# Packing an adjacency matrix on TensorE: 16 columns of whole words, with the rows of a group dealt in another order

## Chip, cores, metric

One core of one Trainium2 chip runs the whole program. The metric is the device time of one execution in microseconds (us). The profiled execution is a separate one, taken with the hardware profiler; its span runs from the first to the last instruction.

## What is computed

Four graph attention layers over N = 8192 nodes with 128 features and one adjacency matrix `adj` of 8192 x 8192 int32 (256 MiB). Each layer normalises x, takes `relu`, and adds an attention output. The first:

```python
h = jnp.maximum(_layernorm(x, axis=-1), 0.0)
Wh = h @ W
e = (Wh @ a1)[:, None] + (Wh @ a2)[None, :]
e = jnp.where(e >= 0, e, ALPHA * e)
scores = jnp.where(adj > 0, e, NEG_BIG)
attention = jax.nn.softmax(scores, axis=1)
x = x + attention @ Wh
```

Layers 1 and 3 end in `elu`. Layer 2 also drops attention weights under 1e-4 and scales by the number of valid neighbours of a row, `L = valid.sum(axis=1)`: this is where the kernel needs degrees of rows.

## The kernel before

**Tiling.** Rows are taken in 16 groups of 512 (`GROUPS`), columns in 64 tiles of 128 (`KT`), which form 4 chunks of 16 tiles (`CHUNKS`, `JC`). For each group and tile VectorE makes q, 128 columns by 512 rows of unnormalised weights (L780), from a mask, and TensorE multiplies four blocks of it with `vals` (128x129, f32) into `acc` (L1240). TensorE runs these products in program order, chunk after chunk, in all four layers.

**The bits.** `adj` is read once, in layer 0, as 512 pieces of 512 KB. From then on the adjacency lies in SBUF as `bits`, one uint16 word for 16 rows of a group: word w (0 to 31, `WORDS`) of column c holds bit b (`PLANES`, 0 to 7) in each of two bytes o, which stands for row 64b + 2w + o of the group. VectorE unpacks a chunk of bits into the byte mask with eight shifts (`planes`, L753).

**How a piece becomes bits.** A piece is 128 rows and 1024 columns (`PT` = 8 tiles). Four pieces (h, o) give the 512 rows of a group over 1024 columns: `adj_pieces` has row 256h + 2p + o on partition p.
1. `load_piece` on SyncE (L432) brings it to one of four slots of `adj_int` (`ADJ_RING`), once ScalarE has read the piece that was there four pieces ago. SyncE issues these loads in the order of pieces, with loads of r and of x, and stores of x, in between (`transfers_and_pieces`).
2. `binary` on ScalarE (L1341) writes 0 or 1 as a byte. Pieces o = 0 and o = 1 interleave, so two of them make one 128x1024 array of 16-bit values, read as f16, in one of four slots of `adj_pairs` (`BIN_RING` / 2). The same instruction sums the row of the piece (`accum_out`), which gives the degree by partition. It may start when the pairs up to eight pieces back are packed.
3. `pack` on TensorE (L1154) multiplies each 128x128 tile of a pair (weights) with the packer. The packer for h is 128x32: row 32m + w has 2^(4h+m) in column w, m = 0 to 3. So a piece of h = 0 gives bits 0 to 3, one of h = 1 bits 4 to 7, and they add up in the same 32 columns of `ps_pack`. A pack is a chunk, 8 pieces: 4 pairs of 8 tiles, 32 matmuls. It waits for each pair as it comes.
4. `words` on ScalarE (L1348) copies `ps_pack` out as uint16.

**What sets the order.** `pack(*ahead(v, c))` stands after chunk c of group v and packs two chunks ahead (`LEAD`); in group 0 packs stand at hand-picked tiles (`FIRST_PACKS`). The last one, of group 15 chunk 3, stands after chunk 1 of group 15; chunks 2 and 3 follow it. TensorE waits in its own order, so a pack whose pair is late holds the chunks behind it.

**Degrees.** `turn_degrees` on SyncE, in layer 1 ahead of the transfers of group 4, writes the 128x64 degrees to DRAM in order of rows (L492), waits, and reads them back by tile (L495). They are read in layer 2. The packer is filled by eight `affine_select` on GpSimd at the start and cleared after the last pack; layer 2 then uses its 128x128 zeros as `nothing`.

Of the kernel before, what the change touches and what calls it, by code (L numbers as in the profile page):

```python
# [7 lines left out]
P = 128  # L8
F = 128
N = 8192  # L10
BLOCKS = 4
# [6 lines left out]
WORDS = W // 16  # L18
# [4 lines left out]
PT = 8  # L23
# [8 lines left out]
PLANES = 8  # L32
# [127 lines left out]
def build(nc, x, adj, ws, avs, out):  # L160
# [11 lines left out]
    wh2 = nc.dram_tensor("wh_of_layer_2", (N, F), F32).ap()  # L172
    rows = nc.dram_tensor("rows", (LAYERS, KT, P), F32).ap()
    rows_by_group = rows.rearrange("k (g b) p -> k g (b p)", b=BLOCKS)
    adj_pieces = adj.rearrange("(g h p o) (k c) -> g k h o p c", h=2, p=P, o=2, c=PT * P)
    degree_rows = nc.dram_tensor("degree_rows", (N,), F32).ap()

    with ExitStack() as ctx:
# [26 lines left out]
        h_total = sb("h_total", [P, 1], F32)  # L205
        h_mean = sb("h_mean", [P, P], F32)
        threshold = sb("threshold", [P, 1], F32)
        packer = sb("packer", [P, BLOCKS, WORDS], F16)
        mean = sb("mean", [P, F], F32)
        s = sb("s", [P, 2, KT + 1], F32)  # L210
        smax = sb("smax", [P, 1], F32)
# [79 lines left out]
        mask_of_unit = flat(adj_int).bitcast(BF16)[:, 0:TRIP * P].rearrange("p (t i) -> p t i", i=P)  # L291
        q_of_unit = flat(q)[:, 0:TRIP * P].rearrange("p (n i) -> p n i", i=P)
        kept_of_unit = flat(q).bitcast(U8)[:, 8 * TRIP * P:9 * TRIP * P].rearrange("p (t i) -> p t i", i=P)
        nothing = packer[:, :, :].rearrange("p b w -> p (b w)")
        counts_of_unit = acc[0][:, 0, F + 1:F + 2]
        r_of_unit, tau_of_unit = rrow[:, 0, 0:P], rrow[:, 0, P:2 * P]

# [124 lines left out]
        def _(sp):  # L422
# [66 lines left out]
            def turn_degrees():  # L489

                sp.wait_ge(degree_ready, 1)
                sp.dma_start(degree_rows.rearrange("(h p o) -> p h o", p=P, o=2),  # L492
                             degree[:, :].rearrange("p (h o) -> p h o", o=2)).then_inc(degree_out, 16)
                sp.wait_ge(degree_out, 16)
                sp.dma_start(degree[:, :], degree_rows.rearrange("(t p) -> p t", p=P), allow_slow_non_contiguous=True)\  # L495
                    .then_inc(degree_in, 16)

# [49 lines left out]
        @block.gpsimd  # L547
        def _(pool):
            nc.gpsimd.memset(ident[:, :], 0.0).then_inc(ident_ready, 1)
            pool.wait_ge(ident_ready, 1)  # L550
            nc.gpsimd.affine_select(out=ident[:, :], in_=ident[:, :], compare_op=ALU.not_equal, fill=1.0,
                                    base=0, pattern=[[-1, P]], channel_multiplier=1).then_inc(ident_ready, 1)
            nc.gpsimd.memset(packer[:, :, :], 0.0).then_inc(consts_ready, 1)
            nc.gpsimd.memset(ones[:, :], 1.0).then_inc(consts_ready, 1)
            nc.gpsimd.memset(threshold[:, :], -0.5).then_inc(consts_ready, 1)
            nc.gpsimd.memset(wh1[:, :, F], 1.0).then_inc(consts_ready, 1)
            pool.wait_ge(consts_ready, 4)
            step = 4
            for h in range(2):
                for m in range(4):  # L560
                    nc.gpsimd.affine_select(out=packer[:, h, :], in_=packer[:, h, :], compare_op=ALU.not_equal,
                                            fill=float(2 ** (4 * h + m)), base=-WORDS * m,
                                            pattern=[[-1, WORDS]], channel_multiplier=1).then_inc(consts_ready, 1)
                    step += 1
                    pool.wait_ge(consts_ready, step)

            for c in range(CHUNKS):
                pool.wait_ge(norm_scales, c + 1)
                for n in range((c + 1) * JC - BLOCKS, (c + 1) * JC):
                    last = nc.gpsimd.tensor_scalar(x_rows_0[:, n, :], x_rows_0[:, n, :], rs_0[:, n:n + 1],  # L570
                                                   nm_0[:, n:n + 1], ALU.mult, ALU.add)
                last.then_inc(norm_by_pool, 1)

            starts = [WHOLE[0], SOON[1], LATE[1], SOON[2], LATE[2]]
            for n, to in enumerate([scales(st)[0][:, :] for st in starts] + [found[:, 0:1], found[:, 1:2], S[:, :]]):
                pool.wait_ge(smax_ready, n + 1)
                nc.gpsimd.partition_all_reduce(to, smax[:, :], P, RMAX).then_inc(S_ready, 1)
                if n == LATE[1].n:
                    for t in range(KT):
                        nc.gpsimd.memset(number[:, t:t + 1], float(t + 1)).then_inc(numbered, 1)  # L580
                    pool.wait_ge(adj_packed, GROUPS * PIECES)
                    nc.gpsimd.memset(packer[:, :, :], 0.0).then_inc(nothing_ready, 1)

        @block.vector
        def _(dve):
# [548 lines left out]
        def _(pe):  # L1134
# [11 lines left out]
            def pack(v, c):  # L1146
# [3 lines left out]
                for i in range(0, QP, 2):  # L1150
                    pe.wait_ge(adj_binary, v * PIECES + (c * QP + i + 2))
                    for t in range(PT):
                        at = (i // BLOCKS * PT + t) * WORDS
                        last = nc.tensor.matmul(ps_pack[:, at:at + WORDS],  # L1154
                                                adj_pairs[:, i % BIN_RING // 2, t * P:(t + 1) * P],
                                                packer[:, i % BLOCKS // 2, :], start=(i == 0 and t == 0),
                                                stop=(i == QP - 2), skip_group_check=True)
                    last.then_inc(adj_packed, 2)

# [519 lines left out]
```

## Time and profile before

| | us |
|---|---|
| median of 3 runs | 3884.77 |
| lowest, highest | 3883.24, 3884.99 |
| the profiled execution | 3884.23 |
| its span | 3882.4 |
| TensorE busy in it | 3819.8 |
| VectorE busy in it | 3570.3 |

The profiled execution has 1.8 us outside its span. Layer 0 takes the first 1055 us or so, the other three layers the rest. Busy time of TensorE counts overlapping matmuls once; durations of single matmuls (176 ns for a pack's) are longer than the distance between their starts, so costs of TensorE are read from the chain or from the distance of starts.

### The profile page before, as it was taken

The numbers are of one execution on the slowest core, as the hardware profiler recorded it, in microseconds if no ns is written. First come the engines' busy times: TensorE is split into PE (matmuls) and PEld (weight loads), VectorE is DVE, ScalarE is ACT, GpSimd is POOL, SyncE is SP. The second block draws the span as 40 slices with busy tenths as digits, with TensorE's granted clock in tenths as the row PEclk, the third lists the DMA queues.
The fourth block names the chain that finished last, engine by engine and source line by source line (L and its number), as shares of the span: only waits on it lengthen the run. The fifth ranks groups of instructions, "written<-read, shape, count | busy, mean of one in ns | idle before, by whom it ended". The sixth has DMA issues, their size and how long they took to land.

```text
span 3882.4 us, 83778 instructions
## 1 busy us (share of the span) xinstructions
PE 3819.8 (98%) x35555; PEld 3810.9 (98%) x35555; DVE 3570.3 (92%) x7790; ACT 1187.1 (31%) x2492; POOL 17.0 (0%) x107
## 2 busy tenths in 40 slices
PE   7999999999999999999999999999997999999999
PEld 6999999999999999999999999999997999999999
DVE  7888989888899999999999999999997999999998
ACT  6766767676631111111133121121122000000000
POOL 1000000000000000000000000000000000000000
PEclk9999999999999999999999999999998999999999
DMA  7888888888401200000002000000000000000000
GB/s 236 294 289 284 286 282 287 286 279 284 146 18 23 18 20 20 18 20 20 15 15 67 18 20 20 18 20 20 18 17 12 17 12 15 17 12 18 15 18 9
DMA packets 207144, 340.05 MB, mean 88 GB/s; under 512 B 56624, under 2 KB 131504, under 8 KB 206768
## 3 DMA queue, kind: packets, MB, share of 16 engines
q1 hardware_dynamic: 205040, 334.41, 27.3%
q8 instruction: 279, 4.57, 0.5%
q14 instruction: 97, 0.79, 0.1%
q10 hardware_dynamic: 1728, 0.27, 0.0%
HBM read 305.57 MB, written 21.20 MB: 84 GB/s over the span
## 4 chain that ended last, share of the span: by engine, by line
PE 95%; ACT 2%; DVE 2%; DMA 1%; issue 0%; ACTq 0%; SPq 0%; DVEq 0%
PE acc L1240 92%; PE ps_pack L1154 1%; PE ps_wh L1258 1%; ACT vals L1436 1%; DVE q L780 1%; ACT adj_pairs L1341 0%; DMA vals<-in_x_dram 0%; PE ps_wh L1252 0%; DVE mask L753 0%; PE acc L1222 0%; DMA adj_int<-in_adj_dram 0%; PE ps_bc L1198 0%; DMA adj_int<-adj_int 0%; PE acc L1177 0%; ACT xnew L1448 0%
## 5 line engine op out<-in xcount | busy, mean ns | idle before, releaser
L1240 PE MATMUL acc<-vals,q 128*128 128x129 f32 (+1 forms) x32576 | 3671.9, 275 | 5.2 <-DVE q L780 5.1
L1240 PEld LDWEIGHTS acc<-vals,q 128*128 128x128 f32 x32576 | 3653.9, 192 | 6.9 <-issue 5.2
L780 DVE SCALAR_TENSOR_TENSOR q<-rrow,R,mask 128x512 f32<-128x512 f32 x3968 | 2825.7, 745 | 172.0 <-PE acc L1240 28.7
L1341 ACT ACTIVATE adj_pairs<-adj_int,threshold 128x1024 uint8<-128x1024 int32 x512 | 585.3, 1146 | 243.9 <-PE ps_pack L1154 143.1
L753 DVE TENSOR_SCALAR mask<-bits 128x512 uint16<-128x512 uint16 x2048 | 435.9, 285 | 7.4 <-DMA rrow<-rows 4.2
L1448 ACT ACTIVATE xnew<-acc,rec 128x128 f32<-128x128 f32 x244 | 69.3, 366 | 854.6 <-DVE rec L818 760.5
L1455 ACT ACTIVATE e<-xnew 128x512 f32<-128x512 f32 x47 | 29.7, 631 | 405.5 <-DVE xnew L849 317.2
L1468 ACT ACTIVATE e<-xnew,nm,rs 128x128 f32<-128x128 f32 x193 | 79.4, 481 | 214.2 <-DVE nm L625 214.2
L1515 ACT ACTIVATE wh<-ps_wh 128x512 f32<-128x512 f32 x48 | 28.7, 598 | 339.9 <-PE ps_wh L1258 339.8
L1463 ACT ACTIVATE sd<-ve 128x4 f32<-128x4 f32 (+1 forms) x49 | 9.9, 202 | 365.6 <-DVE ve L606 365.5
L849 DVE SCALAR_TENSOR_TENSOR xnew<-mean,none,xnew 128x128 f32<-128x128 f32 x188 | 64.9, 345 | 51.2 <-ACT xnew L1448 51.2
L1341 ACT ACTIVATION_READ_ACCUMULATOR adj_pairs<-adj_int,threshold 128x1 f32 x512 | 97.4, 190 | 0.0
L780 DVE SCALAR_TENSOR_TENSOR q<-rrow,tau,mask 128x512 f32<-128x512 f32 x112 | 79.8, 744 | 3.3 <-PE acc L1240 1.6
L1481 ACT ACTIVATE hT<-adj_int 128x512 uint16<-128x512 uint16 x60 | 42.2, 770 | 105.7 <-DMA adj_int<-adj_int 105.7
L1154 PEld LDWEIGHTS ps_pack<-packer,adj_pairs 128*128 128x128 f16 x2048 | 60.8, 96 | 0.9
L1154 PE MATMUL ps_pack<-packer,adj_pairs 128*128 128x32 f16 x2048 | 61.3, 176 | 0.0
L1258 PE MATMUL ps_wh<-w_sb,hT 128*128 128x130 f32 x386 | 52.7, 280 | 2.4 <-ACT hT L1502 1.8
L592 DVE BATCH_NORM_STATS2 stats<-xnew 128x6 f32<-128x128 f32 x193 | 54.4, 283 | 0.1
L1258 PEld LDWEIGHTS ps_wh<-w_sb,hT 128*128 128x128 f32 x386 | 48.0, 195 | 3.3 <-ACT hT L1502 2.5
L1463 ACT ACT_TABLE_LOAD x35 | 44.9, 1283 | 0.6
L1436 ACT ACTIVATE vals<-wh,D 128x129 f32<-128x129 f32 (+1 forms) x128 | 38.0, 393 | 3.7 <-DVE D L713 1.9
L1348 ACT ACTIVATE bits<-ps_pack 128x512 uint16<-128x512 f32 x64 | 36.8, 575 | 0.0
(228 smaller groups left out, 743.9 us busy)
## 6 DMA issues: line engine op xcount, KB each, us to landing
adj_int<-in_adj_dram SPq DMA_DIRECT2D x512, 512.0 KB, 4.9
rrow<-rows SPq DMA_DIRECT2D x60, 256.0 KB, 3.3
x_between_layers<-xnew SPq DMA_DIRECT2D x32, 256.0 KB, 3.4
xin<-x_between_layers SPq DMA_DIRECT2D x32, 256.0 KB, 2.8
xin<-in_x_dram SPq DMA_DIRECT2D x16, 256.0 KB, 5.2
wh_of_layer<-wh SPq DMA_DIRECT2D x1, 4096.0 KB, 16.7
x_of_layer<-xnew SPq DMA_DIRECT2D x16, 256.0 KB, 2.3
xin<-x_of_layer SPq DMA_DIRECT2D x16, 256.0 KB, 2.8
```

The source lines that it names most:

```text
L592: st.did(nc.vector.bn_stats(stats[:, b, :], xnew[:, b, :]))
L753: last = nc.vector.tensor_scalar(mask_words[:, buf, :, b, :], words, amount, ONES, op, ALU.bitwise_and)
L780: nc.vector.scalar_tensor_tensor(q[:, j % RING, :], row, column(R_, t), mask[:, c % 2, j, :], ALU.max, ALU.mult).then_inc(q_ready, 1)
L849: last = nc.vector.scalar_tensor_tensor(o[:, b, :], mean[:, :], none4[:, b:b + 1], o[:, b, :], ALU.mult, ALU.add)
L1154: last = nc.tensor.matmul(ps_pack[:, at:at + WORDS], adj_pairs[:, i % BIN_RING // 2, t * P:(t + 1) * P], packer[:, i % BLOCKS // 2, :], st ...
L1240: last = nc.tensor.matmul(to, q[:, j % RING, b * P:(b + 1) * P], vals[:, t, 0:width(g.layer)], start=first, stop=(t == KT - 1 or g.two and ...
L1258: last = nc.tensor.matmul(projected[:, b // 2, b % 2, :], hT[:, b, :], w_sb[:, g.layer + 1, :], start=True, stop=True)
L1341: nc.scalar.activation(adj_bytes[:, n % BIN_RING // 2, :, n % 2], adj_int[:, n % ADJ_RING, :], ACT.Sign, bias=threshold[:, 0:1], accum_out ...
L1436: last = nc.scalar.activation(vals[:, t, 0:n], wh1[:, t, 0:n], ACT.Copy, scale=scales(st)[4][:, t:t + 1])
L1448: last = nc.scalar.activation(o[:, b, :], acc[g.parity][:, b // 2, at:at + F], ACT.Copy, scale=by[:, b:b + 1])
L1463: nc.scalar.activation(sd[:, m], ve[:, m], ACT.Sqrt).then_inc(sd_ready[g.to], 1)
L1468: last = nc.scalar.activation(h[:, b, :], xnew[:, b, :], ACT.Relu, bias=nm[:, b:b + 1], scale=rs[:, b:b + 1])
```

## The change

A pack matmul streams one packer of 16 columns, `packer[:, 0:16]`, for either h: row 16m + w has 2^m in column w, m = 0 to 7. For that a piece must hold all eight bits of a word: `adj_pieces` now puts row 64m + 32h + 2w + o on partition 16m + w. A piece of h = 0 fills words 0 to 15, one of h = 1 words 16 to 31, each with its eight bits; the two no longer add up in the same columns. The bits in SBUF are the same as before. The load's source is now three dimensions, 8 by 16 by 1024, where it was 128 by 1024. Degrees lie on other partitions, so they are written to DRAM by 16 transfers, each of 16 partitions. The packer's array keeps 128 columns for `nothing`.

```diff
@@ -172,7 +172,8 @@
     wh2 = nc.dram_tensor("wh_of_layer_2", (N, F), F32).ap()
     rows = nc.dram_tensor("rows", (LAYERS, KT, P), F32).ap()
     rows_by_group = rows.rearrange("k (g b) p -> k g (b p)", b=BLOCKS)
-    adj_pieces = adj.rearrange("(g h p o) (k c) -> g k h o p c", h=2, p=P, o=2, c=PT * P)
+
+    adj_pieces = adj.rearrange("(g m h w o) (k c) -> g k h o m w c", m=PLANES, h=2, w=WORDS // 2, o=2, c=PT * P)
     degree_rows = nc.dram_tensor("degree_rows", (N,), F32).ap()
 
     with ExitStack() as ctx:
...
@@ -489,9 +490,13 @@
             def turn_degrees():
 
                 sp.wait_ge(degree_ready, 1)
-                sp.dma_start(degree_rows.rearrange("(h p o) -> p h o", p=P, o=2),
-                             degree[:, :].rearrange("p (h o) -> p h o", o=2)).then_inc(degree_out, 16)
-                sp.wait_ge(degree_out, 16)
+                rows_of_plane = degree_rows.rearrange("(g m h w o) -> m w g h o", m=PLANES, h=2, w=WORDS // 2, o=2)
+                for m in range(PLANES):
+                    for h in range(2):
+                        sp.dma_start(rows_of_plane[m, :, :, h, :],
+                                     degree[m * (WORDS // 2):(m + 1) * (WORDS // 2), :]
+                                     .rearrange("p (g h o) -> p g h o", h=2, o=2)[:, :, h, :]).then_inc(degree_out, 16)
+                sp.wait_ge(degree_out, 16 * PLANES * 2)
                 sp.dma_start(degree[:, :], degree_rows.rearrange("(t p) -> p t", p=P), allow_slow_non_contiguous=True)\
                     .then_inc(degree_in, 16)
 
...
@@ -550,19 +555,19 @@
             pool.wait_ge(ident_ready, 1)
             nc.gpsimd.affine_select(out=ident[:, :], in_=ident[:, :], compare_op=ALU.not_equal, fill=1.0,
                                     base=0, pattern=[[-1, P]], channel_multiplier=1).then_inc(ident_ready, 1)
-            nc.gpsimd.memset(packer[:, :, :], 0.0).then_inc(consts_ready, 1)
+            nc.gpsimd.memset(packer[:, :], 0.0).then_inc(consts_ready, 1)
             nc.gpsimd.memset(ones[:, :], 1.0).then_inc(consts_ready, 1)
             nc.gpsimd.memset(threshold[:, :], -0.5).then_inc(consts_ready, 1)
             nc.gpsimd.memset(wh1[:, :, F], 1.0).then_inc(consts_ready, 1)
             pool.wait_ge(consts_ready, 4)
             step = 4
-            for h in range(2):
-                for m in range(4):
-                    nc.gpsimd.affine_select(out=packer[:, h, :], in_=packer[:, h, :], compare_op=ALU.not_equal,
-                                            fill=float(2 ** (4 * h + m)), base=-WORDS * m,
-                                            pattern=[[-1, WORDS]], channel_multiplier=1).then_inc(consts_ready, 1)
-                    step += 1
-                    pool.wait_ge(consts_ready, step)
+            half = packer[:, 0:WORDS // 2]
+            for m in range(PLANES):
+                nc.gpsimd.affine_select(out=half, in_=half, compare_op=ALU.not_equal, fill=float(2 ** m),
+                                        base=-WORDS // 2 * m, pattern=[[-1, WORDS // 2]],
+                                        channel_multiplier=1).then_inc(consts_ready, 1)
+                step += 1
+                pool.wait_ge(consts_ready, step)
 
             for c in range(CHUNKS):
                 pool.wait_ge(norm_scales, c + 1)
...
@@ -1150,10 +1155,10 @@
                 for i in range(0, QP, 2):
                     pe.wait_ge(adj_binary, v * PIECES + (c * QP + i + 2))
                     for t in range(PT):
-                        at = (i // BLOCKS * PT + t) * WORDS
-                        last = nc.tensor.matmul(ps_pack[:, at:at + WORDS],
+                        at = (i // BLOCKS * PT + t) * WORDS + i % BLOCKS // 2 * (WORDS // 2)
+                        last = nc.tensor.matmul(ps_pack[:, at:at + WORDS // 2],
                                                 adj_pairs[:, i % BIN_RING // 2, t * P:(t + 1) * P],
-                                                packer[:, i % BLOCKS // 2, :], start=(i == 0 and t == 0),
+                                                packer[:, 0:WORDS // 2], start=(i == 0 and t == 0),
                                                 stop=(i == QP - 2), skip_group_check=True)
                     last.then_inc(adj_packed, 2)
 
```

SyncE in layer 0, from the start of the program. A row is one instruction or several alike: line, operation, destination<-source, size of the destination. Before:

```order
L425 DMA vals<-in_x_dram 128x16x128 x2
L432 DMA adj_int<-in_adj_dram 128x1024 x4
L425 DMA vals<-in_x_dram 128x16x128 x2
L432 DMA adj_int<-in_adj_dram 128x1024 x12
L446 DMA xin<-in_x_dram 128x4x128
L432 DMA adj_int<-in_adj_dram 128x1024 x12
```

And now:

```order
L426 DMA vals<-in_x_dram 128x16x128 x2
L433 DMA adj_int<-in_adj_dram 128x1x1024 x4
L426 DMA vals<-in_x_dram 128x16x128 x2
L433 DMA adj_int<-in_adj_dram 128x1x1024 x12
L447 DMA xin<-in_x_dram 128x4x128
L433 DMA adj_int<-in_adj_dram 128x1x1024 x12
```

No load has moved; each has a dimension more, since its source has three.

SyncE in layer 1, ahead of group 4 (`adj_int` serves there as room for a transpose of x). Before:

```order
L446 DMA xin<-x_between_layers 128x4x128
L459 DMA_TRANSPOSE adj_int<-adj_int 128x8x128
L492 DMA degree_rows<-degree 128x32x2
L495 DMA degree<-degree_rows 128x64x1
L469 DMA rrow<-rows 128x512
L450 DMA x_between_layers<-xnew 128x4x128
```

And now:

```order
L447 DMA xin<-x_between_layers 128x4x128
L460 DMA_TRANSPOSE adj_int<-adj_int 128x8x128
L496 DMA degree_rows<-degree 16x16x2 x16
L500 DMA degree<-degree_rows 128x64x1
L470 DMA rrow<-rows 128x512
L451 DMA x_between_layers<-xnew 128x4x128
```

One transfer has become 16 in the same place.

TensorE in a group of layer 0, packs between chunks. Before:

```order
L1154 MATMUL ps_pack<-packer,adj_pairs 128x32 x32
L1240 MATMUL acc<-vals,q 128x129 x64
L1154 MATMUL ps_pack<-packer,adj_pairs 128x32 x32
L1240 MATMUL acc<-vals,q 128x129 x64
L1154 MATMUL ps_pack<-packer,adj_pairs 128x32 x32
```

And now:

```order
L1159 MATMUL ps_pack<-packer,adj_pairs 128x16 x32
L1245 MATMUL acc<-vals,q 128x129 x64
L1159 MATMUL ps_pack<-packer,adj_pairs 128x16 x32
L1245 MATMUL acc<-vals,q 128x129 x64
L1159 MATMUL ps_pack<-packer,adj_pairs 128x16 x32
```

The places and counts are the same, the width is 16 in place of 32. (An f32 matmul of the program runs as two on the engine, so the profile counts 128 for a chunk.)

## Rows read from the trace of the kernel before

**Rows 1.** The page: busy us, share and instructions by engine; 40 slices in tenths

```profile
span 3882.4 us, 83778 instructions
PE 3819.8 (98%) x35555; PEld 3810.9 (98%) x35555; DVE 3570.3 (92%) x7790; ACT 1187.1 (31%) x2492; POOL 17.0 (0%) x107
...
PE   7999999999999999999999999999997999999999
...
DMA  7888888888401200000002000000000000000000
GB/s 236 294 289 284 286 282 287 286 279 284 146 18 23 18 20 20 18 20 20 15 15 67 18 20 20 18 20 20 18 17 12 17 12 15 17 12 18 15 18 9
```

**Rows 2.** The page: the chain that ended last, shares by engine and by line

```profile
PE 95%; ACT 2%; DVE 2%; DMA 1%; issue 0%; ACTq 0%; SPq 0%; DVEq 0%
PE acc L1240 92%; PE ps_pack L1154 1%; PE ps_wh L1258 1%; ACT vals L1436 1%; DVE q L780 1%; ACT adj_pairs L1341 0%; DMA vals<-in_x_dram 0%; PE ps_wh L1252 0%; DVE mask L753 0%; PE acc L1222 0%; DMA adj_int<-in_adj_dram 0%; PE ps_bc L1198 0%; DMA adj_int<-adj_int 0%; PE acc L1177 0%; ACT xnew L1448 0%
```

**Rows 3.** Busy by stretch: layers 0 and 3 (us, engines, clock, DMA, GB/s)

```profile
core 0: us, PE busy (x) PEld busy (x) DVE busy (x) ACT busy (x) POOL busy (x), PEclk, DMA share, GB/s
300.00:420.00 120.00, 120.00 (x1270) 119.90 (x1269) 105.36 (x236) 84.16 (x158) 0.00 (x0) 1.00 0.85 286
...
3000.00:3116.00 116.00, 116.00 (x1041) 116.00 (x1040) 112.31 (x227) 4.80 (x12) 0.00 (x0) 1.00 0.05 15
```

**Rows 4.** The chain in layer 0 in order of time (start, duration, what)

```profile
310.64 0.79 PE ps_pack L1154 x32
311.43 14.39 PE acc L1240 x128
325.82 0.79 PE ps_pack L1154 x32
326.62 14.39 PE acc L1240 x128
```

**Rows 5.** Waits from 300 to 900 us (total, times, longest), SyncE's apart

```profile
ACT adj_pairs L1341 <- DMA adj_int<-in_adj_dram: 60.0, 44, 2.4
...
SPq L432 <- ACT adj_pairs L1341: 475.6, 309, 4.8
```

**Rows 6.** Matmuls of one moving column: line's durations in ns, and the timeline

```profile
L1298 PEld LDWEIGHTS acc<-adj_pairs,adj_int x4: 95/95/98, 2941.8 to 2941.9; 128*128 128x128 bf16 x4
L1298 PE MATMUL acc<-adj_pairs,adj_int x4: 163/164/177, 2941.8 to 2941.9; 128*128 128x1 bf16 x4
...
2941.79 0.17 PEld L1298 LDWEIGHTS acc<-adj_pairs,adj_int 128*128 128x128 bf16 x4 [2.72 <-ACT adj_int L1620]
2941.80 0.25 PE L1298 MATMUL acc<-adj_pairs,adj_int 128*128 128x1 bf16 x4 [2.43 <-ACT adj_int L1620]
```

**Rows 7.** Busy by stretch where the DMA engines are full

```profile
12.00:16.00 4.00, 1.63 (x7) 1.23 (x7) 3.64 (x20) 0.81 (x2) 0.90 (x5) 1.00 1.02 403
...
90.00:100.00 10.00, 10.00 (x116) 9.99 (x116) 10.00 (x17) 6.98 (x12) 0.00 (x0) 1.00 0.98 367
...
310.00:311.00 1.00, 1.00 (x27) 0.99 (x27) 0.86 (x4) 0.07 (x1) 0.00 (x0) 1.00 1.01 401
```

**Rows 8.** Busy by stretch where layer 0's products begin: granted clock before DMA

```profile
60.00:70.00 10.00, 8.73 (x83) 8.75 (x84) 9.63 (x15) 6.45 (x12) 0.00 (x0) 0.71 0.60 212
```

**Rows 9.** Timeline of SyncE's queue at the start (start, us until the last)

```profile
22.86 31.60 SPq L432 DMA_DIRECT2D adj_int<-in_adj_dram  x12
54.50 1.17 SPq L446 DMA_DIRECT2D xin<-in_x_dram  x1
61.49 19.20 SPq L432 DMA_DIRECT2D adj_int<-in_adj_dram  x12
```

**Rows 10.** Timeline of TensorE at the last pack

```profile
1025.60 0.95 PE L1154 MATMUL ps_pack<-packer,adj_pairs 128*128 128x32 f16 x32
1026.38 3.76 PEld L1240 LDWEIGHTS acc<-vals,q 128*128 128x128 f32 x33
```

**Rows 11.** Timeline of SyncE's queue around the degrees in layer 1

```profile
1272.67 0.36 SPq L492 DMA_DIRECT2D degree_rows<-degree  x1
1287.26 0.36 SPq L495 DMA_DIRECT2D degree<-degree_rows  x1
1287.67 4.99 SPq L469 DMA_DIRECT2D rrow<-rows  x1
1309.81 0.38 SPq L450 DMA_DIRECT2D x_between_layers<-xnew  x1
```

**Rows 12.** Loads and binary steps of the pieces: ns min/median/max, landing

```profile
L432 SPq DMA_DIRECT2D adj_int<-in_adj_dram x512: 327/328/4735, 4.3 to 1014.0; - x171
...
DMA to landing us min/median/max: 3.5/4.9/10.2
...
L1341 ACT ACTIVATE adj_pairs<-adj_int,threshold x512: 1134/1142/1292, 21.6 to 1021.4; 128x1024 uint8<-128x1024 int32 x171
```

More of the change, by code:

```diff
@@ L207, in build @@
         threshold = sb("threshold", [P, 1], F32)
-        packer = sb("packer", [P, BLOCKS, WORDS], F16)
+        packer = sb("packer", [P, P], F16)
         mean = sb("mean", [P, F], F32)
@@ L293, in build @@
         kept_of_unit = flat(q).bitcast(U8)[:, 8 * TRIP * P:9 * TRIP * P].rearrange("p (t i) -> p t i", i=P)
-        nothing = packer[:, :, :].rearrange("p b w -> p (b w)")
+        nothing = packer[:, :]
         counts_of_unit = acc[0][:, 0, F + 1:F + 2]
@@ L581, in _ @@
                     pool.wait_ge(adj_packed, GROUPS * PIECES)
-                    nc.gpsimd.memset(packer[:, :, :], 0.0).then_inc(nothing_ready, 1)
+                    nc.gpsimd.memset(packer[:, :], 0.0).then_inc(nothing_ready, 1)
         @block.vector
```

## The prediction

> **What bounds the kernel now.** I read the page first. TensorE is busy 98% of the span, VectorE 92%, and the 40 slices show two parts: in the first ten the DMA engines are busy eight tenths and move about 285 GB/s, after that almost nothing [rows 1]. The chain that ended last is 95% TensorE, and the 2048 pack matmuls are 1% of it [rows 2]. The table by stage says the same: in layer 0 (300 to 420 us) TensorE is busy all the time at full clock, with DMA at 0.85; in layer 3 TensorE is as busy, with DMA at 0.05 [rows 3]. The chain inside layer 0 is nothing but TensorE: a chunk of 128 matmuls takes 14.39 us, a pack of 32 takes 0.79 us [rows 4]. So layer 0 is bound by TensorE, with the stream of adjacency pieces not far behind. The waits show how far: ScalarE waits 60.0 us in 600 for a piece to land, TensorE for none, and SyncE waits 475.6 us for a free slot of the ring [rows 5]. The edit therefore has two prices that count: what a pack costs TensorE, and what a piece costs the DMA engines.
>
> **Part 1, half the columns in a pack.** The number of instructions stays (64 packs of 32 matmuls). A pack is all on the path: 0.79 us / 32 = 24.7 ns from start to start, 64 x 0.79 = 50.6 us in total. Nothing in the trace shows 16 columns of f16. The nearest rows: four matmuls of bf16 weights with one moving column take 0.25 us, the last of them 0.164 us of it, so (0.25 - 0.164) / 3 = 29 ns apart, and their weight loads (0.17 - 0.095) / 3 = 25 ns apart [rows 6]. One column is no cheaper than 32, so what fixes the pitch is not the columns. The other end is that half the columns take half the time: 25.3 us less. I take zero, because the one-column row is the nearer to 16 columns than any proportion is; 0 to -25.3 us is the bound. The Trainium skill ("TensorE: Matmul & The Clock Gate", "Wait — 56ns, not 53.3ns?") has a floor of about 25 ns between starts however few the columns; by that rule this part is worth nothing, while streaming 16 columns less at 2.4 GHz, which is what it counts above the floor, would be 6.7 ns x 2048 = 13.7 us (an estimate).
>
> **Part 2, the dealing of rows.** Each piece is the same 128 rows of 4 KB, and the 512 loads stay where they stand on SyncE. What changes is the form of the load: the source was one dimension of 128 rows by 1024 elements, and is now 8 by 16 by 1024; the built program shows it on the destination, which becomes 128x1x1024. The transfer must be dealt to the 16 DMA engines by some count. If it goes by the 128 partitions, as it can have done before, nothing changes. If it goes by the outermost count that both sides share, only 8 engines get rows, 16 rows each. The trace of before holds no load with an outermost count under 64, so it prices neither; the bounds are zero and the price of 8 engines. I take the 8, since the two sides no longer have the same shape, 8 is the outer count of one of them, and a dealer that wants equal shares on both sides can make 8 and no more. The Trainium skill ("DMA: Bandwidth & Descriptors", "Why a DMA increments its semaphore by 16 and not by 1") states just this: the largest number up to 16 that divides the slowest dimension of both sides, here 8; no row of before can show it, and by any other dealing this part would cost nothing.
>
> The price: 512 KB is 524,288 bytes. With the engines full they move 401 to 403 GB/s (the microsecond after a pack, and 12 to 16 us), a little less at 90 to 100 us: 0.98 and 367 [rows 7]. Half of 401 is 200.5 GB/s, so a piece takes **2.615 us**. A chunk needs eight pieces, 20.9 us, and the other traffic (rows of x, r and the stores: 0.05 of 58 us in a group without pieces, 2.9 us a group [rows 3]) adds 0.7 us: 21.6 us for a chunk. TensorE needs 14.39 + 0.79 = 15.2 us for one. So the DMA engines become the bound of layer 0, and TensorE waits some 6 us in every pack. Such pauses cost clock: after the pause before 60 us the granted clock is 0.71 over ten microseconds [rows 8], that is 5.8 us at the lower level (1.2 of 2.4 GHz), 2.9 us lost. 15.2 + 2.9 = 18.1 us is still under 21.6, so this is hidden in each chunk but the last. ScalarE needs 8 x 1.14 us for a chunk's pieces [rows 12] and is no bound. The ring keeps the engines fed: with TensorE waiting in the pack, all of the next pieces are allowed, and up to four loads stand in the queue.
>
> The sum for layer 0: SyncE has issued 16 pieces by 54.5 us and the 17th goes out at 61.49 us [rows 9]. The 16 take 16 x 2.615 = 42 us and x another 10.5 us, just done by then; for projections that wait on ScalarE behind a late piece I add 4 us (bounds 0 to 10). From 65.5 us: 496 x 2.615 = 1297 us, 16 x 2.9 = 46 us of other traffic, 2 us to land, 1.3 us to make the piece binary, and its pair is packed: 1412 us. Today the last pack starts at 1025.6 and is over at 1026.4 us [rows 10]. In the program's order two chunks follow the last pack in either kernel, and everything behind them is unchanged. So **+386 us, and 3 us** for the cold start of those two chunks.
>
> **Part 3, the rest.** The degrees go out with 16 small transfers in place of one; together they move the same 4096 runs of 8 bytes. SyncE issues at 0.36 us each, so some 6 us more (10 us if an issue is slower). Behind them stand, on SyncE, the load of degrees back, the load of r for group 5 and the store of group 3. Today the first goes out at 1272.67 us, the next store at 1309.81 us: 22 us are free after the load of r at 1287.67 us, and that row is wanted only when the next group begins, about 55 us later [rows 11]. Cost zero; with the cover gone it would be at most 10 us once. Degrees themselves are read in layer 2. A load that needs a longer issue than the 0.328 us of today [rows 12] is hidden too: there are 512 in 1010 us, one in 1.97 us. The packer is made by eight selects on GpSimd as before, each of 16 columns and not 32. Unpacking reads the same words in the same places.
>
> Total against the profiled execution: span 3882.4 + 386 + 3 = 4271 us, with 1.8 us outside the span **4273 us**. That execution (3884.23) stands 0.5 us under the median of the runs, so the prediction needs no shift.
>
> **The rivals.** (a) *Sixteen engines, no gain*: the load is dealt by partitions, pack pitch stays at 24.7 ns. Then nothing on the path changes: 3884 us. For it speaks that the partitions are still 128; against it the mismatch of shapes. (b) *Not slower but faster*: sixteen engines, and the pitch follows the columns. 64 packs at 0.40 us are 25.3 us less, 3859 us; it decides from 0.2% (7.8 us), when a matmul falls under 21 ns. Against it is the one-column row. (c) *Slower with sixteen engines*: the new order of rows hits the memory worse. A piece has 1.97 us, and DMA is busy 0.85 of it, so it costs nothing until transfers are 18% slower, and 10 us for each per cent beyond (512 x 1.97 / 100). Both orders are rows of 32 KB at even steps over most of a group, so I see no reason. (d) *Eight engines at another rate.* If they keep the mean of the busy stretch, 286 / 0.85 / 16 = 21.0 GB/s each, a piece is 3.12 us and the total 4523 us; at 367 GB/s over 0.98 it is 2.80 us and 4365 us; if eight engines disturb each other less than sixteen, 2.45 us gives 4191 us. This is the forecast's own width.
>
> **How the numbers follow.** Eight engines 0.84 (within 4190 to 4460 us: 0.80), (a) 0.12, (b) 0.03, (c) 0.01. The predicted time is that of eight engines. The range is 4190 to 4460 us, and what it leaves out is (a), (b), (c) and the slowest rate of (d). About 0.2% can be told from no change here. Faster 0.03, same 0.12, slower 0.85.
>
> **What would show it.** In the profile after: layer 0 in 14 slices of 40 and not 10; DMA busy there about 0.5 as a mean of sixteen, near 200 GB/s; SyncE's loads 7 us or more to landing, not 4.9; ScalarE waiting for pieces for hundreds of us, TensorE waiting in line L1159 for ScalarE. Pack matmuls 24 to 25 ns apart wherever a pack runs unbroken. Layers 1 to 3 as long as before. Wrong if DMA stays at 0.85 and 285 GB/s (then (a)), or if a pack takes 0.4 us (then (b)).

## The result, and the profile after

| | before | after |
|---|---|---|
| median us (4 runs each) | 3884.88 | 4317.8 |
| lowest, highest | 3883.24, 3885.22 | 4298.87, 4353.05 |
| the profiled execution | 3884.23 | 4298.87 |
| its span | 3882.4 | 4297.1 |

The change makes the kernel slower: ratio 1.1126, 95% interval 1.1104 to 1.1149. The forecast was 4273 us in a range of 4190 to 4460 us.

The page of the kernel after: span, busy time, slices of 107 us each, and the chain that ended last. It answers to [rows 1] and [rows 2].

```profile
span 4297.1 us, 83793 instructions
PE 3956.7 (92%) x35555; PEld 3940.0 (92%) x35555; DVE 3573.6 (83%) x7790; ACT 1217.8 (28%) x2492; POOL 16.8 (0%) x107
...
PE   5778888888777999999999999999999799999999
...
PEclk8898889988888999999999999999999899999999
DMA  5555555555555201000000110000000000000000
...
PE 64%; DMA 28%; issue 3%; ACT 3%; DVE 1%; SPq 0%; ACTq 0%; DVEq 0%
```

TensorE is no longer the whole chain: 28% of it is DMA, where it was 1%. Layer 0 fills thirteen and a half slices, and in them the DMA engines are busy five tenths, not eight. A mean of 0.5 that never rises is what eight full engines out of sixteen look like.

The trace also has a record of every packet of the DMA engines, and a row of a piece is one packet of 4 KB. From 300 to 900 us of the kernel after, eight such packets are under way at once in 72% of the time, and seven to nine in 94%. A packet takes 159 ns in the median, and so it does in the kernel before, which has fifteen to seventeen under way in 58% of the time. One engine thus moves 4096 bytes in 159 ns, 25.8 GB/s, in either kernel; what is new is that only about eight engines carry rows at any moment. No record says which engines they are.

The stretch from 300 to 900 us (columns as in [rows 3]), the waits in it (total, times, longest), and one wait of the whole run:

```profile
300.00:900.00 600.00, 493.06 (x4590) 489.15 (x4587) 384.34 (x842) 317.81 (x569) 0.00 (x0) 0.90 0.53 207
...
ACT adj_pairs L1346 <- DMA adj_int<-in_adj_dram: 283.4, 218, 2.5
...
PE ps_pack L1159 <- ACT adj_pairs L1346: 98.8, 28, 5.1
```

```profile
PE ps_pack L1159 <- ACT adj_pairs L1346: 251.9, 67, 6.1
```

The DMA engines move 207 GB/s in place of 285. ScalarE waits 283.4 us for pieces in these 600 us, where it waited 60.0 in the same stretch of [rows 5]. TensorE waits for ScalarE in the pack, 67 times in the whole run, 3.8 us in the mean; before it did not wait there.

What ScalarE does in one chunk shows the rhythm in which pieces land (its timeline; the bracket is the idle time before, and what ended it):

```profile
521.73 1.15 ACT L1346 ACTIVATE adj_pairs<-adj_int,threshold 128x1024 uint8<-128x1024 int32 x1 [0.79 <-DMA adj_int<-in_adj_dram]
...
524.24 1.15 ACT L1346 ACTIVATE adj_pairs<-adj_int,threshold 128x1024 uint8<-128x1024 int32 x1 [1.27 <-DMA adj_int<-in_adj_dram]
...
526.75 1.15 ACT L1346 ACTIVATE adj_pairs<-adj_int,threshold 128x1024 uint8<-128x1024 int32 x1 [1.27 <-DMA adj_int<-in_adj_dram]
...
530.24 1.15 ACT L1346 ACTIVATE adj_pairs<-adj_int,threshold 128x1024 uint8<-128x1024 int32 x1 [2.24 <-DMA adj_int<-in_adj_dram]
```

Two pieces are mostly 2.51 us apart, now and then longer, as the 3.49 us here. Some of the longer gaps fall where rows of x or r are loaded; this one does not (between the pieces the packet records hold none of either), and its cause is not shown. 524,288 bytes in 2.51 us are 209 GB/s, 26 GB/s for each of eight engines.

The loads by line, to set beside [rows 12], and TensorE's timeline at the last pack, beside [rows 10]:

```profile
L433 SPq DMA_DIRECT2D adj_int<-in_adj_dram x512: 596/596/4617, 4.2 to 1426.7; - x171
```

```profile
1435.16 0.75 PE L1159 MATMUL ps_pack<-packer,adj_pairs 128*128 128x16 f16 x24
...
1437.50 0.36 PE L1159 MATMUL ps_pack<-packer,adj_pairs 128*128 128x16 f16 x8 [1.59 <-ACT adj_pairs L1346]
1437.71 4.60 PE L1245 MATMUL acc<-vals,q 128*128 128x129 f32 x25
```

The last pack is over at 1437.7 us, 411.3 us later than in [rows 10]. From there to the end it is 2859.4 us, before 2856.0. So all of the loss but 3.4 us is in layer 0, ahead of the last pack. The pack also shows how a late pair looks: 24 matmuls run at once, the eight of the last pair 1.59 us later.

### The profile page after: what moved, and what is told of

Same layout as the page of the kernel before. It is cut to its first block, busy times and chain, and to the rows that moved or that the text cites. A ratio compares the mean times of both kernels' runs of the same rounds, so it can differ in the third digit from the quotient of the medians.

```text
span 4297.1 us, 83793 instructions
## 1 busy us (share of the span) xinstructions
PE 3956.7 (92%) x35555; PEld 3940.0 (92%) x35555; DVE 3573.6 (83%) x7790; ACT 1217.8 (28%) x2492; POOL 16.8 (0%) x107
## 4 chain that ended last, share of the span: by engine, by line
PE 64%; DMA 28%; issue 3%; ACT 3%; DVE 1%; SPq 0%; ACTq 0%; DVEq 0%
PE acc L1245 63%; DMA adj_int<-in_adj_dram 28%; ACT adj_pairs L1346 1%; ACT vals L1441 1%; PE ps_wh L1263 1%; DVE q L785 1%; DMA vals<-in_x_dram 0%; PE acc L1182 0%; PE acc L1227 0%; DVE mask L758 0%; SPq L433 0%; ACT e L1473 0%; PE ps_bc L1203 0%; DMA adj_int<-adj_int 0%; ACT xnew L1453 0%
## 5 line engine op out<-in xcount | busy, mean ns | idle before, releaser
L1245 PE MATMUL acc<-vals,q 128*128 128x129 f32 (+1 forms) x32576 | 3789.8, 280 | 19.6 <-DVE q L785 19.3
L1245 PEld LDWEIGHTS acc<-vals,q 128*128 128x128 f32 x32576 | 3771.1, 197 | 22.9 <-DVE q L785 17.2
L1159 PE MATMUL ps_pack<-packer,adj_pairs 128*128 128x16 f16 x2048 | 72.7, 171 | 252.1 <-ACT adj_pairs L1346 251.9
L1159 PEld LDWEIGHTS ps_pack<-packer,adj_pairs 128*128 128x128 f16 x2048 | 66.3, 97 | 259.4 <-ACT adj_pairs L1346 258.4
```

Of the source, the lines that this page charges most:

```text
L1159: last = nc.tensor.matmul(ps_pack[:, at:at + WORDS // 2], adj_pairs[:, i % BIN_RING // 2, t * P:(t + 1) * P], packer[:, 0:WORDS // 2], sta ...
L1245: last = nc.tensor.matmul(to, q[:, j % RING, b * P:(b + 1) * P], vals[:, t, 0:width(g.layer)], start=first, stop=(t == KT - 1 or g.two and ...
```

## Experiments

All kernels compute the whole reference. Times stand beside runs of the kernel before on the same chip (3884 us). The view given of each is the stretch from 300 to 900 us, in layer 0; the last three columns are the granted clock, the busy share of the DMA engines and GB/s. For the kernel before it reads:

```profile
300.00:900.00 600.00, 600.00 (x6312) 599.51 (x6310) 526.25 (x1161) 418.65 (x782) 0.00 (x0) 1.00 0.86 285
```

**e1: sixteen outermost.** On the changed kernel; packer and degrees follow the new partitions.

```diff
-    adj_pieces = adj.rearrange("(g m h w o) (k c) -> g k h o m w c", ...)
+    adj_pieces = adj.rearrange("(g m h w o) (k c) -> g k h o w m c", ...)
```

> The changed kernel with the two inner dimensions of the load swapped: row 64m + 32h + 2w + o goes to partition 8w + m, so the source is 16 by 8 by 1024 and no longer 8 by 16 by 1024. Packer and degrees follow; the result is the reference's. Every piece still holds the same 128 rows, the load still has three dimensions, a pack still streams 16 columns. Theory (eight engines: the load is spread over as many DMA engines as its outermost dimension allows): sixteen engines again, DMA busy 0.85 and 285 GB/s in layer 0, TensorE bound again, 3884 us if a pack's pitch does not depend on its columns, 3859 to 3870 us if it does. Rival (memory: the new set of rows in a piece is read more slowly): the set is unchanged, so 4300 to 4350 us. Rival (issue: a load of three dimensions takes SyncE 0.60 us in place of 0.33 and its descriptors come more slowly): unchanged, 4300 to 4350 us.

Measured: 3996.21 us, ratio 1.0288 (1.0274 to 1.0302).

```profile
300.00:900.00 600.00, 562.14 (x5673) 558.76 (x5672) 481.88 (x1063) 394.24 (x708) 0.00 (x0) 0.97 1.03 257
```

None of the three expectations is met. Both rivals fall as the cause of the main loss: the same rows, three dimensions and the long issue, and 322 of 434 us are gone. But 112 us stay. The DMA engines are full (a share of 1.03: records of neighbouring packets overlap a little) and move 257 GB/s, which is 16 GB/s for each of sixteen; the eight of the changed kernel moved 26 each. By the packet records fifteen to seventeen rows are under way at once in 80% of the time, but a row takes 260 ns in the median and not 159. Here something else slows every row.

**e3: as e1, with 32 columns.** The packer's 16 columns stand in a band of zeros; each matmul takes 32 of it.

```diff
-                                                packer[:, 0:WORDS // 2], ...
+                                                packer[:, band:band + WORDS], ...
```

> As e1_sixteen_outermost, but each pack matmul streams 32 columns of the packer again, 16 of them zeros (the 16 packer columns stand in the middle of a band of zeros, so both h add up in the same 32 columns). The only difference from e1 is the width. Theory (a pack matmul is held by a pitch of 25 ns whatever its width up to 32): within 2 us of e1. Rival (the pitch follows the columns): e1 is 14 us (streaming alone) to 25 us (half the pitch) faster than this one.

Measured: 4002.4 us, ratio 1.0293 (1.0272 to 1.0315), against 1.0288 of e1. The medians are 6 us apart, more than the 2 us expected, but the runs of either lie from 3981 to 4006 us, so no difference is seen. Since DMA bounds both, this settles less on the pitch than was meant; e8 and e10 do that.

**e2: the changed kernel, with 32 columns.** The same band of zeros, the load left at 8 by 16 by 1024.

> The changed kernel with 32 columns in a pack again (16 of them zeros), the load left at 8 by 16 by 1024. Eight engines: the whole loss is in the load, so as the changed kernel, 4300 to 4350 us. Rival (something in the narrow pack costs: writes to separate halves of the words, or packs that TensorE runs late): back towards 3884 us.

Measured: 4308.99 us, ratio 1.1077 (1.1049 to 1.1106). The narrow pack has no part in the loss that the spread of these runs (4285 to 4353 us) would show.

**e4: four outermost.** The kernel before, pieces dealt so that the outermost count is 4; packer and degrees follow.

```diff
-    adj_pieces = adj.rearrange("(g h p o) (k c) -> g k h o p c", h=2, p=P, o=2, c=PT * P)
+    adj_pieces = adj.rearrange("(g j h w o) (k c) -> g k h o j w c", j=4, h=2, w=WORDS, o=2, c=PT * P)
```

> The kernel before (packs of 32 columns), but a piece takes the rows 128j + 64h + 2w + o, j = 0 to 3, w = 0 to 31, so the load's source is 4 by 32 by 1024; packer and degrees follow and the result is the reference's. Eight-engines theory, carried on: four engines, a piece takes 524,288 bytes / 100 GB/s = 5.23 us and 0.09 us for the other traffic, 495 of them from about 125 us on: the last pack ends near 2780 us, the whole takes 5600 to 5700 us, DMA busy about 0.27 and 103 GB/s in layer 0. Rivals (the new rows, or three dimensions, are slow by themselves): about as the changed kernel, 4300 us, since the rows are as far apart and the dimensions as many.

Measured: 5519.94 us in one run. The page's slices of layer 0 and the loads:

```profile
DMA  3222222222222222222001000010000000000000
...
L432 SPq DMA_DIRECT2D adj_int<-in_adj_dram x512: 528/529/5626, 4.0 to 2638.5; - x171
```

DMA busy is 0.27 and 108 GB/s from 300 to 900 us. A load goes out every (2638.5 - 4.0) / 511 = 5.16 us, in the changed kernel every (1426.7 - 4.2) / 511 = 2.78 us. Half the outermost count, half the rate; the packet records have four rows under way at once in 87% of the time, at 159 ns in the median. So the count limits the engines. The total is 80 us under the lower expectation: from the 17th load on, at 93.3 us and not 125, loads go out every (2638.5 - 93.3) / 495 = 5.14 us, where the expectation had 5.32. The Trainium skill has the rule ("DMA: Bandwidth & Descriptors", "Why a DMA increments its semaphore by 16 and not by 1"): up to sixteen engines, the largest number that divides the slowest dimension of both sides. These runs agree with it at 4 and at 8.

**e6: the kernel before, long issue.** One switch of the builder, nothing else: no transfer is marked for the short issue.

> The kernel before with one switch of the builder: no transfer is marked for SyncE's short issue path, so that each load is issued in the long way, as loads of three dimensions are (0.54 to 0.60 us on SyncE in place of 0.33). Its source keeps two dimensions and its rows. Theory (memory, as above): one issue in 1.97 us is hidden, 3884 us within 3 us. Rival (the long issue gives descriptors late): part or all of e1's loss, up to 3996 us.

Measured: 3884.28 us, ratio 1.0002 (0.9993 to 1.0011).

```profile
L434 SPq DMA_DIRECT2D adj_int<-in_adj_dram x512: 471/472/4310, 3.9 to 1014.3; - x171
```

An issue of 0.472 us in place of 0.328 costs nothing. It is not quite the 0.537 us of e1; e11 and e13 below issue in 0.535 us and lose nothing either. For the 0.596 us of the changed kernel, one in 2.78 us, this is an argument and not a test of its own.

**e5: sixteen outermost, near rows.** The changed kernel, h moved to another bit of the word.

```diff
+    adj_pieces = adj.rearrange("(g n h w o) (k c) -> g k h o n w c", n=2 * PLANES, h=2, w=WORDS // 4, ...)
```

> The changed kernel, but h is another bit of the row: row 32n + 16h + 2w + o, n = 0 to 15, w = 0 to 7, on partition 8n + w. The source is 16 by 8 by 1024, the packer is unchanged (16 columns, whole words), the words go to ps_pack in two runs of eight; degrees follow and the result is the reference's. Sixteen engines as in e1_sixteen_outermost, the load has three dimensions and the slow issue as there. What differs from e1: the eight rows of one engine are 64 KB apart, as before, where in e1 they are 2 MB apart. Theory (the 112 us that e1 keeps over the kernel before are memory: rows of a large pitch in one engine's hand are read slowly): DMA back at 0.85 and 285 GB/s, 3884 us, within 5 us. Rival (form: a load of three dimensions is dealt to partitions in a way, or described so slowly, that 256 GB/s is its limit): DMA at 1.0 and 256 GB/s as in e1, 3996 us.

Measured: 4004.74 us, ratio 1.0319 (1.0303 to 1.0336).

```profile
300.00:900.00 600.00, 554.69 (x5629) 550.70 (x5628) 475.63 (x1049) 389.93 (x701) 0.00 (x0) 0.97 1.03 254
```

The theory of memory falls: rows 64 KB apart in the inner dimension are read at the same 16 GB/s for each engine as rows 2 MB apart (266 ns a row in the median, 260 in e1).

**e9: the rows of before, in three dimensions.** The kernel before; each piece holds the same 128 rows, dealt in another order. The packer keeps 32 columns.

```diff
+    adj_pieces = adj.rearrange("(g h b a o) (k c) -> g k h o a b c", h=2, b=8, a=16, o=2, c=PT * P)
```

> The kernel before with the same 128 rows in each piece, dealt so that the load needs three dimensions: row 256h + 32b + 2a + o on partition 8a + b, a = 0 to 15 outermost, b = 0 to 7. Packer (32 columns) and degrees follow; the result is the reference's. Theory (form): three dimensions alone bring what e1 and e5 show, DMA at 1.0 and 256 GB/s, near 4000 us. Rival (rows): the rows of a piece are those of before, so 3884 us.

Measured: 4001.05 us, ratio 1.0309 (1.0292 to 1.0325).

```profile
300.00:900.00 600.00, 569.62 (x5817) 566.39 (x5816) 489.11 (x1068) 402.36 (x719) 0.00 (x0) 0.98 1.03 262
```

Which rows a piece holds plays no part (a row takes 255 ns in the median here); what e1, e5 and e9 have in common is the shape 16 by 8 by 1024.

**e8: whole words from rows at one step.** The changed kernel with h as the lowest bit of the word. The load is of two dimensions again, and the packer is the changed kernel's.

```diff
+    adj_pieces = adj.rearrange("(g p h o) (k c) -> g k h o p c", p=P, h=2, o=2, c=PT * P)
...
-                        at = (i // BLOCKS * PT + t) * WORDS + i % BLOCKS // 2 * (WORDS // 2)
-                        last = nc.tensor.matmul(ps_pack[:, at:at + WORDS // 2],
+                        at = (i // BLOCKS * PT + t) * WORDS + i % BLOCKS // 2
+                        last = nc.tensor.matmul(ps_pack[:, at:at + WORDS - 1:2],
```

> The changed kernel, but h is the lowest bit of the word: row 4p + 2h + o on partition p. A piece again holds all eight bits of 16 words (every second word), the packer is the same 128x16, but the 128 rows of a load stand at one step, so its source is 128 by 1024 as in the kernel before. Words go to ps_pack at a step of two; degrees go out in one transfer; the result is the reference's. Theory (form: what e1 and e5 lose is the load of three dimensions, whatever its rows): two dimensions give DMA 0.85 and 285 GB/s, TensorE bound, 3884 us if the pitch of a pack does not depend on columns, 14 to 25 us less if it does. Rival (rows: pieces that take rows from all over the group are read slowly): as e1 and e5, near 4000 us.

Measured: 3884.37 us (11 runs), ratio 1.0000 (0.9991 to 1.0009).

**e10: as e8, with 32 columns.**

> As e8_one_step_narrow, but a pack matmul streams 32 columns, 16 of them zeros. The only difference is the width, and TensorE is the bound in both. Theory (25 ns from start to start at 16 as at 32 columns): within 2 us of e8. Rival (the pitch follows the columns): 14 to 25 us above e8.

Measured: 3884.57 us (11 runs), ratio 1.0000 (0.9991 to 1.0010). Both are bound by TensorE, so here the two widths can be compared: the intervals reach some 4 us either way, and the rival asks for 14 us at least. A pack of 32 matmuls on TensorE's timeline, first e8, then e10:

```profile
311.17 0.95 PE L1155 MATMUL ps_pack<-packer,adj_pairs 128*128 128x16 f16 x32
311.97 0.58 PE L1241 MATMUL acc<-vals,q 128*128 128x129 f32 x3
```

```profile
311.74 0.96 PE L1156 MATMUL ps_pack<-packer,adj_pairs 128*128 128x32 f16 x32
312.54 0.58 PE L1242 MATMUL acc<-vals,q 128*128 128x129 f32 x3
```

In either the next product starts 0.80 us after the pack, 25 ns a matmul. Only the last matmul's own end is earlier, by 0.01 us. The intent of the change is here in full (whole words, 16 columns), without its load, and no gain is seen.

**e11: 64 by 2.** The changed kernel, h as the second bit of the word; three dimensions, sixteen engines.

```diff
+    adj_pieces = adj.rearrange("(g n h w o) (k c) -> g k h o n w c", n=64, h=2, w=2, o=2, c=PT * P)
```

> The changed kernel, but h is the second bit of the word: row 8n + 4h + 2w + o, n = 0 to 63, w = 0 or 1, on partition 2n + w. The source is 64 by 2 by 1024, three dimensions as in e5 (16 by 8), and as near to the single step of e8 as three dimensions can be; 16 columns, the result is the reference's. Theory A (any load of three dimensions with sixteen engines runs at 256 GB/s, by the way in which its parts are dealt or described): 3985 to 4010 us, DMA 1.0 and 256 GB/s in layer 0. Theory B (it depends on how many rows follow each other in the inner dimension, eight in e1, e5 and e9): two rows give less loss, 3884 to 3940 us.

Measured: 3885.24 us, ratio 1.0002 (0.9992 to 1.0011), with 0.85 and 285 GB/s. A row takes 159 ns in the median, as before. Three dimensions are not slow by themselves, which also corrects the theory of e9.

**e13: 32 by 4.**

> Between e5 (16 by 8 by 1024) and e11 (64 by 2 by 1024): h is the third bit of the word, row 16n + 8h + 2w + o, n = 0 to 31, w = 0 to 3, on partition 4n + w, source 32 by 4 by 1024. Sixteen engines, 16 columns, the result is the reference's. Theory A (an outermost count of exactly sixteen leaves each engine one contiguous run of eight partitions, any larger one spreads them): full speed as e11, 3885 us. Theory B (the loss grows with the inner count, eight in e5 and two in e11): between the two, DMA near 270 GB/s, 3890 to 3970 us.

Measured: 3884.48 us, ratio 1.0001 (0.9991 to 1.0010).

```profile
300.00:900.00 600.00, 599.62 (x6285) 599.04 (x6284) 525.30 (x1159) 419.87 (x781) 0.00 (x0) 1.00 0.84 284
```

A row takes 159 ns in the median here too, so no slower DMA hides behind TensorE. The loss does not grow with the inner count step by step: at 4 there is none, at 8 it is 112 us. As a piece has 128 rows in all of them, an outermost count of sixteen and an inner count of eight come together, and these runs cannot say which of the two matters. An inner count of sixteen or more with fewer engines (the changed kernel, e4) leaves a row at 159 ns.

**e12: two pieces in a load.**

> The kernel before with pieces o = 0 and 1 brought by one load of 1 MB into two slots: 256 source rows in one run of steps, destination 128 partitions by 2 by 1024. Half the loads, each of three dimensions on the destination's side only; the ring is two loads deep in place of four, so that some time is lost by that alone. What is read is the rate per busy share in layer 0, not the total. Theory A (unequal shapes of the two sides are dealt the slow way): 256 GB/s at a share of 1.0, 16 GB/s for each engine. Theory B (only a source of three dimensions is slow): 21 to 24 GB/s for each engine while busy, as before.

Measured: 4024.8 us in one run, 0.78 and 248 GB/s: 248 / 0.78 / 16 = 19.9 GB/s for each engine while busy, where before has 20.7 and e1 has 15.6. The rate is near that of before, and a row takes 159 ns in the median, so it speaks against Theory A. TensorE and the DMA engines both have idle time, as fits a ring of two loads; that the ring is the cause was not tried.

The pieces in one table, by the shape of the load's source:

| source | kernel | DMA share, GB/s | us |
|---|---|---|---|
| 128 by 1024 | before, e6, e8, e10 | 0.85 to 0.86, 285 | 3884 |
| 64 by 2 by 1024 | e11 | 0.85, 285 | 3885 |
| 32 by 4 by 1024 | e13 | 0.84, 284 | 3884 |
| 16 by 8 by 1024 | e1, e3, e5, e9 | 1.03, 254 to 262 | 3996 to 4005 |
| 8 by 16 by 1024 | after, e2 | 0.53, 205 to 207 | 4318, 4309 |
| 4 by 32 by 1024 | e4 | 0.27, 108 | 5520 |

The first three rows are bound by TensorE, so their rates say that DMA is fast enough there, not how fast it could be.

## Why the prediction was right, step by step

**What bounds the kernel.** Right. Taking the DMA engines' reserve away moved layer 0, and no edit of the pack moved anything.

**Part 1, the pack at zero.** Right. e8 against e10 puts 16 columns against 32 with the same load: 3884.37 and 3884.57 us. The one-column matmuls of [rows 6] were the right neighbours. The bound of 25.3 us, and the 13.7 us of streaming, are not there. The Trainium skill ("TensorE: Matmul & The Clock Gate", "Wait — 56ns, not 53.3ns?") gives a floor of about 25 ns between starts; the 25 ns of both widths agree with it.

**Part 2, eight engines.** Right; the eight packets under way at once show it, and e1 and e4 show that it follows the outermost count. That eight and not sixteen engines would work was forecast from the form of the load, with no row to show it. The runs leave no other cause for the larger part: the rows of a piece (e1, which has the same), three dimensions (e11, e13) and the narrow pack (e2) are each excluded, and the issue takes 0.537 us in e1 and 0.596 here.

**The price.** The terms of the sum in the profiled execution:

| term | forecast | measured |
|---|---|---|
| the 17th load goes out | 65.5 us | 78.5 us |
| one load to the next, with other traffic | 2.71 us | (1426.7 - 78.5) / 495 = 2.72 us |
| last pack over | 1412 us | 1437.7 us |
| TensorE for a chunk and its pack, cold starts included | 18.1 us | 493.06 / (600 / 21.8) = 17.9 us, projections of x included |
| from the last pack to the end, more than before | 3 us | 3.4 us |
| span | 4271 us | 4297.1 us |

The rate of the stream was met within 0.6 per cent, but by luck, since two errors cancel: a piece alone takes 2.51 us, not 2.615, and all that comes on top is 0.21 us for each piece, not 0.09. The start was mis-sized by 13 us. It had 4 us for late pieces, but x itself came later: its two last loads, behind four loads of pieces, kept SyncE until 28.5 us, before until 18.2 (first line, of the kernel before; then the kernel after):

```profile
10.66 7.49 SPq L425 DMA_DIRECT2D vals<-in_x_dram  x2
...
11.41 17.04 SPq L426 DMA_DIRECT2D vals<-in_x_dram  x2
28.51 42.62 SPq L433 DMA_DIRECT2D adj_int<-in_adj_dram  x12
```

In [rows 9] the twelve pieces go out from 22.86 to 54.46 us, here until 71.1. The last pack is 26 us late. 13 of them are the start, 7 are 0.015 us more on each of 495 loads, and 5 are the end: the last load went out at 1426.7 us and was packed 11.0 us later, where the sum had one more step of 2.7 us and 3.3 us behind it. It let a load begin to move as it goes out, but others stand in the queue ahead of it. The median lies 19 us above the profiled execution, which no term of the sum foresaw; the runs of this kernel spread over 54 us, those of before over 2.

**Part 3.** Right that it is hidden, though an issue of the degrees took longer than either figure given: 11.74 us for sixteen.

```profile
1687.66 11.74 SPq L496 DMA_DIRECT2D degree_rows<-degree  x16
1707.17 0.38 SPq L500 DMA_DIRECT2D degree<-degree_rows  x1
1707.60 4.90 SPq L470 DMA_DIRECT2D rrow<-rows  x1
1725.20 0.38 SPq L451 DMA_DIRECT2D x_between_layers<-xnew  x1
```

The load of r goes out 17.6 us before the next store, 22.1 us in [rows 11].

**The signs.** Slices, busy share, rate and the wait in L1159 came as named. The profile gives no landing times for these loads, but the chain goes from an issue to its landing, and its steps between 490 and 690 us are 8.7 to 10.2 us, over the 7 named:

```profile
512.95 8.76 DMA adj_int<-in_adj_dram
...
523.00 9.73 DMA adj_int<-in_adj_dram
```

One number did not come: the wait of TensorE in a pack is 3.8 us and not some 6. The prediction had the reason itself, a chunk of 18.1 us in 21.6, which leaves 3.5 us, but took the wait from 15.2. The cost of the clock was well met:

```profile
518.24:535.45 17.21, 17.21 (x134) 17.20 (x131) 6.01 (x8) 8.12 (x14) 0.00 (x0) 0.83 0.52 206
```

This chunk, after a pause of 3.54 us, has a granted clock of 0.83 over 17.21 us, so 5.9 us at the lower level and 2.9 us lost (forecast 5.8 and 2.9).

**The rivals.** Rival (c), slower with sixteen engines, was given 0.01, and its only cause was memory. Its reason against was also misread: before, the rows of a piece are 64 KB apart over half a group, now they come in eight runs of sixteen over nearly all of it. With a shape of 16 by 8 the rival is real, 112 us (e1), only by another cause than the rows. Had the change had that shape, the same reasoning would have missed, as the expectation of e1 did; that it had 8 by 16, where a row stays at 159 ns, is luck. Its point of decision, transfers 18% slower, fits what came in kind: with rows at 260 ns and not 159, 257 GB/s at full engines is too little for the 285 that TensorE asks for.

## What to carry to other kernels

Look at the outermost count of both sides of every large load, after any rearrangement of rows: in these runs it decided how many DMA engines work, and eight and four of them moved 207 and 108 GB/s. If the rows must be dealt anew, look for an order with one step (e8), or one whose outermost count is a multiple of sixteen and above it (32 in e13, 64 in e11). And before narrowing a small matmul, compare the distance of starts with that of the narrowest one in the trace: here one column stood at 29 ns and 32 at 25 ns, and half the columns bought nothing.

## What was not expected of the hardware

- A load of 16 by 8 by 1024 gives 254 to 262 GB/s with all engines busy (1.03), where 32 by 4 and 64 by 2 give what TensorE asks for, 284 to 285 GB/s at 0.84 to 0.85. Each of sixteen engines moves 16 GB/s, against 26 at eight, and a row of 4 KB takes 255 to 266 ns in the median (e1, e3, e5, e9), against 159 in all other kernels here. The rows and their distance do not matter (64 KB, 1 MB and 2 MB apart: e5, e9, e1).
- Why is open. One idea fits but was not tried: at sixteen each engine may write one run of eight neighbouring partitions, so that two engines meet at one entrance to SBUF. The Trainium skill ("SBUF — State Buffer", "Door 1: The DMA port swizzle (why `[64,N]` ≈ `[32,N]`)") gives such a map, with four neighbouring partitions to a port and 32 further the same port again; no run here shows which engine wrote which partitions, the idea needs the rows of 32 by 4 to be dealt in some other way, and eight engines, which may have runs of sixteen partitions, did not suffer from it (159 ns).
- The kernels bound by the DMA engines repeated less well: 54 us between four runs of the changed kernel and 11 to 28 us in e1, e2, e3, e5 and e9, against 2 to 5 us for those bound by TensorE.
- SyncE takes 0.596 us to issue a load of 8 by 16, 0.537 us for 16 by 8, 0.535 us for 32 by 4 and 64 by 2, 0.472 us for 128 rows without the short issue (e6) and 0.328 us with it. No run shows that any of it cost time.
